# A 192-wide query rank cut into 128 + 64 instead of 96 + 96, and a feed-forward network whose first weights are asked for on two queues

## What is computed

```python
q_lat = rmsnorm(hidden_states @ q_a_w, q_a_norm_w)              # rank 192
q = (q_lat @ q_b_w).reshape(b, s, H, QKD)                       # 32 heads of 128 + 64
ckv = hidden_states @ kv_a_w
kv_lat, k_pe = (ckv[..., :KV_RANK], ckv[..., KV_RANK:])         # rank 64
kv = (rmsnorm(kv_lat, kv_a_norm_w) @ kv_b_w).reshape(b, s, H, NOPE + VD)
scores = (q_nope . k_nope + rope(q_pe) . rope(k_pe)) * QKD ** -0.5
# an indexer keeps the best 128 keys of each query; softmax; times v; @ o_w
# the gated network, every weight with a low-rank addition of rank 16:
h1, h3 = _lora_linear(x, w1, A1, B1), _lora_linear(x, w3, A3, B3)
g = silu(h1) * h3
out = _lora_linear(g, w2, A2, B2)
```

## Time and profile before

| | us |
|---|---|
| median of three runs | 1817.47 (1814.63 to 1821.27) |
| the profiled execution's own time | 1820.58 |
| its span, first to last instruction | 1818.5 |
| PE busy | 1680.2 (92% of the span) |
| DVE busy | 1085.9 (60%) |
| ACT busy | 848.9 (47%) |
| POOL busy | 708.4 (39%) |

### The profile page before, as it was taken

How to read it: one execution, slowest core, us unless ns; L and a number is a source line. 1 busy time by engine, 2 the same in 40 slices (tenths; PEclk the granted TensorE clock), 3 DMA queues, 4 the chain that set the end, 5 groups by cost and what they waited for, 6 DMA issues and landing times. The chain is left out here.

```text
span 1818.5 us, 27417 instructions
## 1 busy us (share of the span) xinstructions
PE 1680.2 (92%) x8938; PEld 1237.8 (68%) x8938; DVE 1085.9 (60%) x2474; ACT 848.9 (47%) x1608; POOL 708.4 (39%) x735
## 2 busy tenths in 40 slices
PE   6799995999978999999999999689989999999998
PEld 5588884888757666766666766477765555468886
DVE  3456658999527667777667777335657677510222
ACT  3455654444316555555545555344125556653321
POOL 1112222454646556666556566186001121222221
PEclk9899997999988999999999999999969999999999
DMA  8422222220110000100000000165432243131111
GB/s 225 152 80 60 79 74 74 60 66 24 47 32 5 17 17 17 33 17 17 17 17 17 33 17 12 41 214 174 143 52 52 54 79 70 45 99 59 44 49 47
DMA packets 108156, 110.48 MB, mean 61 GB/s; under 512 B 39008, under 2 KB 70208, under 8 KB 108032
## 3 DMA queue, kind: packets, MB, share of 16 engines
q1 hardware_dynamic: 105984, 105.25, 20.9%
q10 hardware_dynamic: 2048, 3.67, 0.6%
HBM read 81.34 MB, written 27.39 MB: 60 GB/s over the span
## 5 line engine op out<-in xcount | busy, mean ns | idle before, releaser
L1312 POOL TENSOR_SCALAR a_p<-a_p,a_rinv 128x640 f32<-128x640 f32 (+7 forms) x256 | 190.3, 746 | 174.5 <-DVE a_rinv L1238 173.5
L1269 ACT ACTIVATE a_p<-a_sm,a_nmax 128x640 f32<-128x640 f32 (+7 forms) x256 | 198.6, 777 | 106.3 <-DVE a_nmax L1230 103.4
L1230 DVE CUSTOM_DVE_ANT_0 a_sm<-ps,maskb 128x640 f32<-128x640 f32 (+7 forms) x256 | 192.5, 752 | 92.2 <-PE ps L1174 88.6
L2122 DVE CUSTOM_DVE_ANT_0 ga_sm<-ps,strip 128x640 f32<-128x640 f32 (+1 forms) x224 | 163.2, 754 | 85.3 <-PE ps L2029 83.7
L2142 ACT ACTIVATE ga_pt<-ps 128x1024 f32<-128x1024 f32 (+1 forms) x192 | 148.0, 810 | 113.6 <-PE ps L2052 112.9
L1186 PE MATMUL ps<-ident,a_p 128*128 128x128 f32 x1152 | 173.2, 276 | 12.1 <-DVE a_pt L1245 11.9
L1186 PEld LDWEIGHTS ps<-ident,a_p 128*128 128x128 f32 x1152 | 133.7, 141 | 35.0 <-DVE a_pt L1245 11.2
L2182 POOL TENSOR_SCALAR_AFFINE_SELECT ga_pt<-ga_pt 128x512 f32<-128x512 f32 x64 | 40.6, 635 | 292.4 <-ACT ga_pt L2142 292.3
L1201 PE MATMUL ps<-a_pt,vst 128*64 128x512 f32 (+3 forms) x768 | 150.8, 502 | 1.8 <-DVE a_pt L1245 1.1
L1281 ACT COPY a_pt<-ps 128x512 f32<-128x512 f32 x128 | 74.2, 579 | 164.6 <-PE ps L1186 109.4
L1174 PE MATMUL ps<-kh,lq_qh 128*128 128x512 f32 (+3 forms) x384 | 132.1, 398 | 14.0 <-DVE a_nmax L1230 10.0
(11 more groups left out here) (314 smaller groups left out, 4047.8 us busy)
## 6 DMA issues: line engine op xcount, KB each, us to landing
ctx_d<-a_ctxst SPq DMA_DIRECT2D x16, 512.0 KB, 3.0
ctxn<-ctx_d SPq DMA_DIRECT2D x32, 256.0 KB, 3.5
ctxn<-wvo_d SPq DMA_DIRECT2D x32, 256.0 KB, 4.6
ga_qst<-qkd SPq DMA_DIRECT2D x42, 128.0 KB, 4.7
f_wr<-in_L_ffn_w SPq DMA_DIRECT2D x20, 256.0 KB, 2.5
x<-in_L_attn_hidden_states SPq DMA_DIRECT2D x16, 256.0 KB, 4.0
op_wo<-in_L_attn_o_w SPq DMA_DIRECT2D x8, 512.0 KB, 6.4
ix_w<-in_L_attn_idx_wq_w SPq DMA_DIRECT2D x64, 64.0 KB, 1.9
```

Of the source, the lines that this page charges most:

```text
L1230: dve.tensor_tensor_reduce(out=sm[kind][:, 0:w], in0=slots[kind][:, 0:w], in1=maskb[:, MASK_OFF[t]:MASK_OFF[t + 1]], scale=-scale, scalar= ...
L1269: act.activation(p[kind][:, v // 2 % 2, 0:w], sm[kind][:, 0:w], ACT.Exp, bias=nmax[:, v % 4:v % 4 + 1], scale=-1.0, accum_out=rsum[:, v % ...
L1312: pool.tensor_scalar(mine, mine, rinv[:, v % 4:v % 4 + 1], 1.0, ALU.mult, ALU.mult).then_inc(norm_done, 1)
L2122: dve.tensor_tensor_reduce(out=sm[kind][:, 0:w], in0=slots[kind][:, 0:w], in1=strip[:, S - w:], scale=-1.0, scalar=3.0e38, op0=ALU.add, op ...
```

## The change

**The rank is cut at 128.** `QC` = 96 gives way to `QCH` = (128, 64). The latent of the queries is now one tile `xq` of three parts: part 0 is the high part of the first 128 rows, part 2 their low part, and part 1 holds the other 64 rows twice: their high part on partitions 0 to 63, their low part on 64 to 127. For that, the opening writes the last 64 columns of the latent twice before it turns them. The folded weight is loaded to match, its last 64 rows twice. One product over 128 rows then gives high·high and high·low of the rest together, and a piece is five products. The fifth has 64 contracted rows, for which the program names a tile of 64x128.

```diff
@@ latent_queries, pe_piece
-            for h in range(2):
-                ins = mm3(pe, ps[:, bank_of(pair, k), :], (wh[:, h, a], wl[:, h, a]), (qlh[:, h, at], qll[:, h, at]),
-                          h == 0, h == 1)
+            n = QR - P
+            parts = ((wh[:, 0, a], xq[:, 0, at]), (wh[:, 0, a], xq[:, 2, at]), (wl[:, 0, a], xq[:, 0, at]),
+                     (wh[:, 1, a], xq[:, 1, at]), (wl[0:n, 1, a], xq[0:n, 1, at]))
+            for h, (left, right) in enumerate(parts):
+                ins = pe.matmul(ps[:, bank_of(pair, k), :], left, right, start=h == 0, stop=h == len(parts) - 1,
+                                skip_group_check=True)
@@ latent_queries, load_weights
-            sp.dma_start(wraw[:, :, :, :].rearrange("p c b n -> p (c b n)"), wabs_d[pair]).then_inc(raw_in, 16)
+            n = QR - P
+            sp.dma_start(wraw[:, 0].rearrange("p a n -> p (a n)"), wabs_d[pair][0:P, :]).then_inc(raw_in, 16)
+            for r0 in (0, n):
+                sp.dma_start(wraw[r0:r0 + n, 1].rearrange("p a n -> p (a n)"), wabs_d[pair][P:QR, :]).then_inc(raw_in, 16)
@@ opening, turn_w (the indexer's turn_fold likewise)
                     for a in range(2):
-                        for k in range(2):
-                            at = (2 * a + k) * QC
-                            ins = pe.transpose(ps[:, bank_t, at:at + QC], wq[:, s, k, a * QKD:a * QKD + NOPE],
-                                               ident[0:QC, 0:QC])
+                        for k, n in enumerate(QCH):
+                            at = a * QR + k * P
+                            ins = pe.transpose(ps[:, bank_t, at:at + n], wq[0:n, s, k, a * QKD:a * QKD + NOPE],
+                                               ident[0:n, 0:n])
@@ opening, fold (the indexer's fold likewise)
                     for a in range(2):
-                        for k in range(2):
-                            at = (2 * a + k) * 64
-                            pe.matmul(ps[0:QC, bank_abs, at:at + 64], wTq[:, s, a, k], wTkv[:, s, 0, a * 64:a * 64 + 64],
-                                      start=True, stop=True)
+                        for k, n in enumerate(QCH):
+                            at = (2 * k + a) * 64
+                            pe.matmul(ps[0:n, bank_abs, at:at + 64], wTq[:, s, a, k * P:k * P + n],
+                                      wTkv[:, s, 0, a * 64:a * 64 + 64], start=True, stop=True)
@@ opening, DVE
+                    dve.scalar_tensor_tensor(out=ql[:, t, QR:], in0=lat[:, t, P:QR], scalar=rs[:, 0, t:t + 1],
+                                             in1=qn[:, P:], op0=ALU.mult, op1=ALU.mult)
...
-                    dve.tensor_tensor(qll[:, :, at], ps[0:QC, b, 2 * P:].rearrange("p (k n) -> p k n", k=2),
-                                      f32(qlh[:, :, at]), ALU.subtract).then_inc(lo_done, 1)
+                    dve.tensor_tensor(xq[:, 2, at], ps[:, b, 2 * P:3 * P], f32(xq[:, 0, at]), ALU.subtract)
+                    low = xq[QR - P:, 1, at]
+                    dve.tensor_tensor(low, ps[QR - P:, b, 3 * P:], f32(low), ALU.subtract).then_inc(lo_done, 1)
```

```diff
@@ lora_ffn, SP
+                first_w(0)
+                sp.wait_ge(zero, START + 1)
+                first_b(0)
+                first(1)
+                first(2)
                 sp.wait_ge(zero, START + 4)
-                first(0)
-                for r in COPIES:
-                    sp.dma_start(a13[r, 0], A1).then_inc(a_in, 16)
-                    sp.dma_start(a13[r, 1], A3).then_inc(a_in, 16)
-                first(1)
                 for r in COPIES:
                     sp.dma_start(b2[:, :, r], B2.rearrange("(k p) r -> p k r", p=P)).then_inc(b2_in, 16)
-                first(2)
                 second(0)
@@ lora_ffn, PE
                 turn(0)
+                turn(1)
+                pe.wait_ge(a13_low, START + 1)
+                fold(0)
+                turn(2)
+                pe.wait_ge(a13_low, START + 2)
+                fold(1)
                 pe.wait_ge(b2_in, START + 48)
                 ...
                 ins.then_inc(b2_turned, 1)
-                turn(1)
-                pe.wait_ge(a13_low, START + 1)
-                fold(0)
-                turn(2)
-                fold(1)
                 turn(3)
@@ lora_ffn, ACT
+                act.wait_ge(zero, START + 2)
+                for m, (A, landed) in enumerate(((A1, a1_in), (A3, a3_in))):
+                    for r in COPIES:
+                        act.dma_start(a13[r, m], A).then_inc(landed, 16)
                 bring_b(0)
-                act.wait_ge(a_in, START + 96)
-                act.copy(a13s[:, :, :], a13).then_inc(a13_high, 1)
+                for m, landed in enumerate((a1_in, a3_in)):
+                    act.wait_ge(landed, START + 48)
+                    act.copy(a13s[:, m], a13[:, m]).then_inc(a13_high, 1)
```

More of the change, by code:

```diff
@@ L202, in _ @@
                 sp.dma_start(strip[:, :], strip_d).then_inc(strip_in, 16)
-                ix["landed"] = [(strip_in, 16)] + [(out[k], 16 * len(range(k, NP, NS))) for out in (abs_out, vo_out)
-                                                   for k in range(NS)]
+                ix["landed"] = [(strip_in, 16)] + [(out[k], n * len(range(k, NP, NS)))
+                                                   for out, n in ((abs_out, 32), (vo_out, 16)) for k in range(NS)]
             @block.tensor
@@ L564, in copy_rotary @@
                 def copy_rotary(i):
-                    pool.wait_ge(fqkv_in, START + i * 48 + 48)
-                    pause(pool, abs_out, i * 16, rot_passed)
-                    for a in range(2):
-                        pair = fq[:, :, a * QKD + NOPE:(a + 1) * QKD].rearrange("p c (n e) -> p c e n", e=2)
-                        pool.tensor_copy(wabs[:, :, a, 64:96], pair[:, :, 0, :])
-                        ins = pool.tensor_copy(wabs[:, :, a, 96:128], pair[:, :, 1, :])
+                    pool.wait_ge(fqkv_in, START + i * 64 + 64)
+                    pause(pool, abs_out, i * 32, rot_passed)
+                    for k, n in enumerate(QCH):
+                        pair = fq[0:n, k].rearrange("p (a m) -> p a m", a=2)[:, :, NOPE:].rearrange(
+                            "p a (n e) -> p a e n", e=2)
+                        pool.tensor_copy(wabs[0:n, k, :, 64:96], pair[:, :, 0, :])
+                        ins = pool.tensor_copy(wabs[0:n, k, :, 96:128], pair[:, :, 1, :])
                     ins.then_inc(rot_done, 1)
@@ L592, in turn_fold @@
                     for a in range(2):
[L593 to L595 removed]
+                        for k, n in enumerate(QCH):
+                            at = a * QR + k * P
+                            pe.transpose(ps[:, 4, at:at + n], fq[0:n, k, a * QKD:a * QKD + NOPE], ident[0:n, 0:n])
                     pe.transpose(ps[:, 5, 0:P], fkv[:, 0:NOPE], ident[:, :])
@@ L601, in fold @@
                     for a in range(2):
-                        for k in range(2):
-                            at = 2 * P + (2 * a + k) * 64
-                            pe.matmul(ps[0:QC, 5, at:at + 64], fTq[:, a, k], fTkv[:, 0, a * 64:a * 64 + 64], start=True,
-                                      stop=True)
+                        for k, n in enumerate(QCH):
+                            at = 2 * P + (2 * k + a) * 64
+                            pe.matmul(ps[0:n, 5, at:at + 64], fTq[:, a, k * P:k * P + n], fTkv[:, 0, a * 64:a * 64 + 64],
+                                      start=True, stop=True)
                     pe.wait_ge(fo_in, START + i * 16 + 16)
@@ L784, in _, with first_w @@
             def _(sp):
-                def first(u):
+                def first_w(u):
                     k, m = divmod(u, 2)
@@ L856, in fold2 @@
                         pe.wait_ge(w2f_done, START + k)
+                    else:
+                        pe.wait_ge(b2_low, START + 1)
                     for j in range(DT):
@@ L1416, in act_weights @@
         def act_weights(act, pair, first=False):
-            act.wait_ge(raw_in, START + pair * 16 + 16)
+            act.wait_ge(raw_in, START + pair * 48 + 48)
             if not first:
```

140 lines of the change are left out of this document (73 added, 67 removed).

## The result

The changed kernel takes 1830.91 us (median of five runs, 1829.11 to 1832.33), the kernel before 1817.47 beside it (five runs). The ratio is 1.0072, with a 95% interval of 1.0052 to 1.0091: slower by some 13 us, where 12.5 was forecast (1830.0 for the median). The profiled execution of after has a span of 1829.7 us against 1818.5.

A forecast was written before the change was run, and what follows sets the result against it. TensorE was taken as the bound, busy 1680 of 1818.5 us. Opening +5.5, indexer +7.2, network -5.0, head of attention +0.8 and attention +4.0 sum to +12.5: 1830.0 us on the 1817.5 median, range 1804 to 1836.

The forecast's parts named there:

- The cost of a change of tile: On TensorE, each change between the full tile and half of it costs 0.20 us, with bounds 0 and 0.20.
- the second rival: Every change of tile costs only the 0.09 us pause, no weight load exposed: sum -2.2, 1815.3 us; chance 0.15.
- Folding: Eight pairs in the opening, eight in the indexer stage: six tile changes at 0.15, 0.9 us a pair; indexer +7.2.
- The head of attention: Start of attention: SP's extra DMA issues add 0.9 us, the first half-clock piece gains 0.1; net +0.8.
- Attention: Attention rounds: tile changes cost more than the saved products, +0.28 us a round, +0.68 in the first; +4.0 taken.
- The wait of 0.47: Attention, behind the piece at step 7: PE's wait for VectorE absorbs a little of +4.6, leaving +4.0 us.
- The opening: Opening stage: folding's tile changes, partly covered by waits, and one more subtraction per token tile; +5.5 us.
- ACT's second store per pair: Opening: an issue of some 0.4 us, covered by PE's longer work; uncovered, up to three pairs at 0.4 each.
- One more subtraction per token tile: Opening, on the latent: the added subtraction per token tile costs 0.3 us in all.
- The cover that was named for VectorE's eight scalings: Opening: eight more scalings, some 0.22 us each, 1.8 in all, covered because PE reaches that point later by more.
- The network: Head of the gated network: six fewer issues on SP's queue (2.9 us) and an earlier start (2.0); -5.0 us.
- the third rival: Network head: ACT hands over factor B too late, half of the 5 us is lost: 1832.5 us; chance 0.05.

The follow-up runs named there:

- the kernel with full tiles: Changed kernel with folding on full tiles (two heads' rests side by side) and the fifth product over all 128 rows: 1805.12 us, ratio 0.9916 to the kernel before.

## Why the prediction was right

Point by point, by its own steps.

- **The cost of a change of tile: right.** Forecast 0.20 from the 0.09 of the earlier trace rows and the 0.11 of the earlier trace rows, measured 0.19 for a cut by rows, built up as told: a pause of 0.09 and a load of 0.10 that isn't hidden. That load puts the second rival, the pause alone, out as well. Putting a cut by rows beside a cut by output columns held. The Trainium skill's rule ("TensorEngine Tiling (Array Packing)", Key Properties: a change of the tiling mode drains TensorE) agrees with the pause of 0.09 at 64x128, and the run with two products of 64 rows shows that it is the change that is paid. The Trainium skill, "TensorE: Matmul & The Clock Gate", Part 3, The mechanism, says that a weight load is pulled ahead of the running product when the row groups don't conflict, or when it goes to the background weight buffer. Here both hold rows 0 to 63, and the load stayed exposed. The row groups alone don't explain it: the load of a full product conflicts with the full product ahead of it just as much, and it is done ahead (704.51, for the product at 704.75). Why the load isn't done ahead across a change of tile, no run shows.
- **Folding: right.** 0.9 us a pair was forecast and 0.84 measured (six changes at 0.14 each). The indexer stage grew by 7.2 us in the first profile and 6.3 by the second, forecast 7.2.
- **The head of attention: right.** +0.8 forecast, +0.5 measured.
- **Attention: wrong, by its rounds in sign too.** The failing step is "The wait of 0.47 takes up a little, so I take +4.0". I counted PE's own work (+0.28 a round forecast, +0.21 measured: 2 x 0.15 less 2 x 0.045) and let one wait take a crumb of it. In fact both pieces with more work have a wait for VectorE behind them, and the one of 0.17 behind step 10 I hadn't put among the rows. VectorE's part starts at the end of the piece, which came 0.04 us earlier. The round got 0.18 shorter: -2.7 us over 15 rounds instead of +4. The trace of before held all of it.
- **The opening: direction right, size off.** Forecast +5.5, measured +7.7 by the first profiles and +8.7 by both. The first profile of before is short of full clock between 20 and 40 us (0.91); against its second, which isn't, the two of after are 9.8 to 9.9 longer. The part ahead of the latent was sized well: from the start of the projection to the indexer's first products lie four pairs and the waits that they eat, 30.98 us in the execution of before that has no half clock there and 33.53 in after, and the next pair cost 0.85: 3.4 for the five, forecast 3.7. The failing steps are two. "ACT's second store per pair ... is covered by PE's longer work" named its price without the cover, three pairs at 0.4, and the cover wasn't there: it cost 0.65 in the one place where it can be read alone, and taking it out gave 3.4 us back. "One more subtraction per token tile adds +0.3" for all eight tiles was 0.31 for a single one where it can be read alone, and taking it out gave 2.3 back. Both stand in a chain in which PE idles. After the longer idle time PE stayed at half clock, for which the forecast had nothing and which is worth 2.7 us. The parts overlap and don't add up to the 5.8. The cover that was named for VectorE's eight scalings did hold: they ended at 66.05 us and PE came at 66.98. In the kernel with full tiles PE came first and waited 0.51 for them.
- **The network: right in kind, a fifth to a third too much.** -5.0 forecast, -3.2 in the first profile; `up(0)` came 3.4 nearer there and 4.1 on average. The 2.0 us of the earlier start came in full (1.9 us behind the barrier instead of 3.9). The six issues brought 0.8 instead of 2.9 up to unit 4, because three of the remaining ones took 0.94 to 1.32 us instead of 0.43. The loads of SP's queue stayed last, so the third rival's mechanism, ACT handing over too late, didn't occur.

The errors of attention (6.7 too high by the rounds) and of the opening and network (2 to 4 and 1 to 2 too low) cancelled, with 4.2 us of clock at the end of attention on one side and 2.6 us behind attention on the other in the profiled execution.

## What to carry to other kernels

Count the changes of tile, not the products: each change between the full array and a tile of 64 rows or 64 output columns cost 0.14 to 0.19 us here. So trading a full product for one of half the rows is a loss between full products (0.38 paid, 0.23 saved), and hardly a gain where a change stands there anyway (0.19 paid, 0.23 saved). The half rows are better filled with whatever stands there (a second-order term, the other head's rest). Where another engine stands behind a group of products, price the group by when it ends and look for every wait behind it. Before calling a DMA issue covered, follow the issuing engine's own order to the next engine that waits for it.

## What the runs showed that I had not expected

- A product over 128 rows was faster in place than the same over 64: 0.23 us to its follower against 0.42.
- Idle time can be paid twice. In the opening PE idled for 3.4 us and then ran at half clock for 27 us (in the second profile with a break at 80 to 84 us), which cost 2.7 us up to the fifth turn alone. Work that nothing reads, put into the wait, kept the clock at full speed; put where the wait had become shorter than it, it cost what it lasted.
- Single DMA issues on SyncE take 0.8 to 2.3 us instead of 0.43. At the head of the network they were 21 of 446, none of them among the 66 ahead of unit 4 in before, and three at the same places in both profiles of after. A term made of issue times carries that as an uncertainty of one to three microseconds.
